# Local attention: one output projection for two units, bias products over the full height, transposes and low part moved, two mask copies on VectorE

## The chip, the core and the metric

The kernel runs on one core of a Trainium2 chip. A core has TensorE (PE, matrix products into PSUM), VectorE (DVE), ScalarE (ACT), GpSimd (POOL) and SyncE (SP, which issues DMAs). Each engine works through its own queue in order; between engines there are only semaphores. The metric is device time in microseconds, lower is better.

## The reference

Two layers, each a cross-attention and a feed-forward network, on `x` of shape (16, 64, 512). Only the first, the local attention, is touched:

```
x = x + _L0_xattn_ref(_layernorm(x, axis=-1), ctx_4096, Wq, bq, Wk, bk, Wv, bv, Wo, bo)

B, C, T = x.shape                      # 16, 64, 512
H, W = (HEADS, WINDOW)                 # 8, 16
q = _pointwise(Wq, bq, x)              # einsum('oc,bct->bot', W, t) + b
k = _pointwise(Wk, bk, cond)
v = _pointwise(Wv, bv, cond)
k = jnp.pad(k, ((0, 0), (0, 0), (pad_left, pad_right)))      # 8 and 7
v = jnp.pad(v, ((0, 0), (0, 0), (pad_left, pad_right)))
idx = jnp.arange(T)[:, None] + jnp.arange(W)[None, :]
dots = jnp.einsum('bhdt,bhdtw->bhtw', qh, k_win) * scale
attn = jax.nn.softmax(dots, axis=-1)
out = jnp.einsum('bhtw,bhdtw->bhdt', attn, v_win)
return _pointwise(Wo, bo, out)
```

Behind it come a gated feed-forward network, a cross-attention of 32 heads and a routed feed-forward network. The gated one begins with the layer norm of the rows that local attention leaves, transposed.

## The kernel before

`X` lies in SBUF as eight tiles; a tile holds two batches, 2 x 64 channels, on the 128 partitions, and 512 time steps. A tile has four units of 128 time steps, so there are 32 units, and each unit has eight blocks of 16 time steps with the 32 keys that their windows touch.

`window_attention` is a pipeline written out by hand: step n does something for several units at once, on each engine in the order in which `step` is written. With q = n mod 4 (called step 0 to step 3 of a tile here):

- TensorE: in step 0 the query projection of the next tile (L404), in step 1 its key projection (L392), both into the bank `PJ`; in step 3 four transposes of the layer-normed row of the tile t - 2 for the next stage (L233), also into `PJ`. Then in every step: value products of unit n - 3 (L444, two of 128 columns), and for the first and last unit of a tile, at the edge of the time axis, one more with `less` and `bv_row`, of one partition (L446), that takes the bias out of padded keys; the mask and score products of unit n (L451, L457), the output projection of unit n - 5 (L481, four of 128 columns), and the products of probabilities and values of unit n - 4 (L493).
- VectorE: transposition of scores to keys (L587), maximum (L590), the add into `X` with the output bias (L599); a step later sum (L566) and reciprocal (L571), another step later the transposition of probabilities (L580). Besides, per tile: layer-norm statistics of finished rows in step 1 (L198), the normed row at the start of step 2 (L222, `norm.normalise`, into `qT`), the normed `xn` for a later query projection at the start of step 3 (L528), and the low part of the transposed row at the end of step 3 (L245, `norm.low`).
- GpSimd: subtraction of the maximum (L663), product with the reciprocal (L670).
- ScalarE: exponential (L707), copies of values and of heads out of PSUM (L701, L731), biases, the high part of the transposed row (L239), and the masked copies of the query, eight per tile, one per head, from `qp` into `qx` (L722; three in step 1, three in step 2, two in step 3).

Value products and output projection share PSUM bank 6 (`VT`, `AO`), so the next value product waits for the X add (`x_added`). The query projection waits for the low part (`low_done`), since both use `PJ`. The diff touches `window_attention` alone.

Of the kernel before, what the change touches and what calls it, by code (L numbers as in the profile page):

```python
# [279 lines left out]
def window_attention(nc, sh, d, norm, ffn):  # L280
# [9 lines left out]
    STEPS = (-4, UNITS + 6, 8, UNITS_PER_TILE)  # L290
    HH = WH // 2
    FIRST = 2
    SHARERS = 3
    with ExitStack() as st:
# [17 lines left out]
        less = sb("wa_less", [1, 2, P])  # L312
        bv_row = sb("wa_bv_row", [1, P])
# [4 lines left out]
        oh = sb("wa_oh", [P, 2, HH, UNIT_T])  # L318
# [8 lines left out]
        AO = sh.PS[:, 6, 256:256 + UNIT_T]  # L327
# [3 lines left out]
        def context_due(n):  # L331
# [6 lines left out]
                 "q_mm k_mm q_biased q_ready k_ready edges bv_loaded sc_mm masks_ready keyed maxed subbed exped summed recip probs "  # L338
# [3 lines left out]
        with nc.Block() as block:  # L342
            @block.sync
            def _(sp):
                def load(dst, name, done, a, b):
                    sp.dma_start(dst[:, a:b, :], d[name][2 * a:2 * b, :, :].rearrange("(t b) s e -> (b s) t e", b=2)
                                 ).then_inc(done[a], 16)

                load(sh.X, "x", x_loaded, *LOADS[0])
                sp.dma_start(sh.const[:], d["consts"][:, :C_BASE]).then_inc(S["const_loaded"], 16)  # L350
                for i, w in enumerate(("Wq", "Wk", "Wv", "Wo")):
                    sp.dma_start(wrow[:, i, :], d["L0_" + w]).then_inc(S["loaded"], 16)
                    sp.dma_start(brow[i:i + 1, :], d["L0_b" + w[1]].rearrange("(a c) -> a c", a=1)).then_inc(S["loaded"], 16)
                load(sh.CTX, "ctx", ctx_loaded, *LOADS[0])
                for b2 in range(2):
                    sp.dma_start(bv_row[:, b2 * SEQ:(b2 + 1) * SEQ], d["L0_bv"].rearrange("(a c) -> a c", a=1)
                                 ).then_inc(S["bv_loaded"], 16)
# [12 lines left out]
            def _(pe):  # L370
# [23 lines left out]
                def step(n, u, t):  # L394
# [18 lines left out]
                    if q == 3 and live(t - 2, TT - 1):  # L413
                        if live(t + 1, TT):
                            pe.wait_ge(S["k_ready"], t + 2)
                        else:
                            pe.wait_ge(norm.low_done, t - 1)
                        norm.transpose(pe, t - 2, u // 4, PJ)

                    if live(n, UNITS):  # L420
                        pe.wait_ge(S["q_ready"], t + SHARERS)
                        pe.wait_ge(S["k_ready"], t + 1)
                        if not isinstance(n, int) or n >= 1:
                            pe.wait_ge(S["keyed"], n)
                        else:
                            pe.wait_ge(S["masks_ready"], 2)

                    m, w = n - 3, (u - 3) % 8
                    if live(m, UNITS):
# [7 lines left out]
                        if not isinstance(n, int) or m >= 3:  # L437
                            pe.wait_ge(S["x_added"], m - 2)
# [25 lines left out]

                    m = n - 4
# [6 lines left out]
                    m = n - 5  # L472
                    if live(m, UNITS):
                        pe.wait_ge(S["oh_copied"], m + 1)
                        pe.wait_ge(S["vt_copied"], m + 3 if live(m + 2, UNITS) else UNITS)
                        if not isinstance(n, int) or m >= 1:
                            pe.wait_ge(S["x_added"], m)
# [32 lines left out]
            def _(vec):  # L510
# [43 lines left out]
                def step(n, u, t):  # L554
# [6 lines left out]
                    if q == 1 and live(t - 2, TT - 1):  # L561
                        vec.wait_ge(S["x_added"], 4 * t - 4)
# [31 lines left out]
                    m, w = n - 5, (u - 5) % 4  # L594
                    if live(m, UNITS):
                        vec.wait_ge(S["ao_mm"], m + 1)
                        x = sh.X[:, bass.ds(t - 1 if q >= 1 else t - 2, 1),
                                 w * UNIT_T:(w + 1) * UNIT_T]
                        nc.vector.scalar_tensor_tensor(x, AO.rearrange("p (a e) -> p a e", a=1), bias[:, 3:4], x,  # L599
                                                       ALU.add, ALU.add).then_inc(S["x_added"], 1)  # L600

# [16 lines left out]
            def _(gp):  # L618
# [6 lines left out]
                nc.gpsimd.memset(wT[:], 0.0).then_inc(S["zeroed"], 1)  # L625
                nc.gpsimd.memset(blank[:], 0.0).then_inc(S["zeroed"], 1)
# [6 lines left out]
                nc.gpsimd.memset(less[:, 0, 0:PAD], -1.0).then_inc(S["padded"], 1)  # L633
                nc.gpsimd.memset(less[:, 1, P - PAD:], -1.0).then_inc(S["padded"], 1)
# [47 lines left out]
            def _(act):  # L682
# [8 lines left out]
                def step(n, u, t):  # L691
# [17 lines left out]
                    if live(t + 1, TT):  # L709
                        if q == 0:  # L710
                            if isinstance(t, int) and t == 0:
                                act.wait_ge(S["q_ready"], SHARERS)
                            add_bias(t + 1, 0, "q_mm", qp[:], "q_biased")
# [13 lines left out]
                    if live(m, UNITS):  # L727
                        act.wait_ge(S["oh_mm"], m + 1)
                        if not isinstance(n, int) or m >= 2:
                            act.wait_ge(S["ao_mm"], m - 1)  # L730
                        nc.scalar.activation(oh[:, u % 2, :, :].rearrange("p h (i x) -> p i h x", i=4),  # L731
# [1325 lines left out]
```

## Time and profile before

| | us |
|---|---|
| median of 3 runs | 1130.06 (1130.03 to 1131.46) |
| the profiled execution | 1132.62 |
| its span in the profile | 1130.8 |
| TensorE busy | 1045.0 (92%) |
| VectorE busy | 661.4 (58%) |
| GpSimd busy | 514.7 (46%) |
| ScalarE busy | 352.3 (31%) |

Local attention ends at 173.3 us, and the rest of the span belongs to the three later stages. In the rows further down, a timeline row gives the start and the length in us, the engine, the source line, the operation, what it writes and reads, and in brackets how long its engine stood idle before it and what ended that. PEld is the load of stationary operands. An f32 product appears in two records for each instruction. The start of an instruction can lie a little before the end of the one before it on the same engine, so distances between starts say what an instruction costs its engine.

### The profile page before, as it was taken

What the parts mean: (1) busy time and instruction counts of PE and PEld (TensorE: products, weight loads), DVE (VectorE), ACT (ScalarE), POOL (GpSimd) and SP (SyncE); (2) the same over time, 40 slices, a digit from 0 to 9 for tenths busy, and PEclk for the clock granted to TensorE, in tenths of its full rate; (3) what the DMA queues carried; (4) which work ended last, traced back from release to release, by engine and by line L of the source; (5) the groups of instructions that cost most, each with busy time, mean ns of one, the idle gap of its engine ahead of it and who ended that gap; (6) DMA issues with size and microseconds to landing.
All of it is one profiled execution on the core that took longest, in us unless ns stands there. A gap on an engine that the chain in (4) does not pass through costs nothing. (4 is left out here: it accounts for less than half of the span.)

```text
span 1130.8 us, 24015 instructions
## 1 busy us (share of the span) xinstructions
PE 1045.0 (92%) x9170; PEld 869.1 (77%) x9170; DVE 661.4 (58%) x1357; ACT 352.3 (31%) x826; POOL 514.7 (46%) x594
## 2 busy tenths in 40 slices
PE   6899988999999889999999999999999999745993
PEld 3677777888887678888888888888888888534783
DVE  4799873544544675656555565656555666741324
ACT  3677743222222323222222222222222222211331
POOL 3555531422123365445454454444544442337755
PEclk9899998999999889999999999999999999976997
DMA  7100006656450021111011110011010000036768
GB/s 237 23 3 4 4 4 177 209 192 212 151 205 30 29 72 33 47 29 48 29 33 51 31 46 30 29 48 29 28 57 29 29 10 1 1 129 213 242 215 270
DMA packets 51806, 92.07 MB, mean 81 GB/s; under 512 B 10748, under 2 KB 24316, under 8 KB 51260
## 3 DMA queue, kind: packets, MB, share of 16 engines
q1 hardware_dynamic: 42108, 69.13, 19.4%
q10 hardware_dynamic: 6624, 12.06, 3.1%
q0 software_dynamic: 2976, 9.44, 2.5%
q8 instruction: 76, 1.25, 0.5%
q14 instruction: 22, 0.18, 0.0%
HBM read 77.25 MB, written 36.18 MB: 100 GB/s over the span
## 5 line engine op out<-in xcount | busy, mean ns | idle before, releaser
L121 PE MATMUL PS<-NTh,W 128*128 128x256 f32 (+2 forms) x688 | 217.1, 315 | 0.0
L122 PE MATMUL PS<-NTl,W 128*128 128x256 f32 (+2 forms) x688 | 214.2, 311 | 0.0
L123 PE MATMUL PS<-NTh,W 128*128 128x256 f32 (+2 forms) x688 | 214.2, 311 | 0.0
L122 PEld LDWEIGHTS PS<-NTl,W 128*128 128x128 f32 (+1 forms) x688 | 131.3, 191 | 7.0
L123 PEld LDWEIGHTS PS<-NTh,W 128*128 128x128 f32 (+1 forms) x688 | 129.4, 188 | 8.6
L121 PEld LDWEIGHTS PS<-NTh,W 128*128 128x128 f32 (+1 forms) x688 | 129.6, 188 | 7.2
L1507 POOL TENSOR_TENSOR W<-ca_raw,W 128x512 fp32r<-128x512 f32 x64 | 82.6, 1292 | 109.7 <-ACT W L1354 109.7
L1445 DVE TENSOR_REDUCE ca_su<-room 128x4 f32<-128x256 f32 x64 | 26.8, 419 | 154.0 <-ACT room L1379 154.0
L1474 DVE TENSOR_TENSOR room<-PS,ca_sinT 64x512 f32<-64x512 f32 (+1 forms) x192 | 115.0, 599 | 2.6
L121 PE MATMUL PS<-W,ca_aTh 128*128 128x512 f32 x256 | 106.9, 417 | 3.1 <-DVE X L1462 3.1
L122 PE MATMUL PS<-W,ca_aTh 128*128 128x512 f32 x256 | 101.3, 396 | 0.0
L123 PE MATMUL PS<-W,ca_aTl 128*128 128x512 f32 x256 | 100.9, 394 | 0.0
L1379 ACT ACTIVATE room<-room 128x256 f32<-128x256 f32 x64 | 26.8, 419 | 227.1 <-POOL room L1557 227.1
L1547 POOL TENSOR_TENSOR qT<-room 128x512 f32<-128x512 f32 x64 | 81.7, 1277 | 29.1 <-DVE room L1474 27.7
L1474 DVE TENSOR_TENSOR room<-PS,ca_cosT 128x512 f32<-128x512 f32 (+1 forms) x96 | 57.8, 602 | 56.8 <-PE PS L1293 56.4
L1044 POOL TENSOR_TENSOR ff_hl<-ff_hf,W 128x512 fp32r<-128x512 f32 (+1 forms) x22 | 28.6, 1302 | 132.9 <-ACT W L939 132.9
L1000 DVE TENSOR_TENSOR X<-X,PS 128x512 f32<-128x512 f32 x88 | 60.3, 686 | 48.8 <-PE PS L123 48.3
L1403 ACT ACTIVATE room<-PS 128x256 f32<-128x256 f32 x64 | 24.6, 385 | 186.1 <-PE PS L1319 186.1
L121 PE MATMUL PS<-ca_wkvh,CTh 128*128 128x256 f32 x256 | 79.3, 310 | 2.2 <-issue 2.2
L1534 POOL TENSOR_TENSOR room<-room,ca_rc 128x256 f32<-128x256 f32 x64 | 39.3, 613 | 76.7 <-DVE ca_rc L1447 76.7
L123 PE MATMUL PS<-ca_wkvh,CTl 128*128 128x256 f32 x256 | 72.4, 283 | 0.0
L122 PE MATMUL PS<-ca_wkvl,CTh 128*128 128x256 f32 x256 | 72.1, 282 | 0.0
(253 smaller groups left out, 2354.4 us busy)
## 6 DMA issues: line engine op xcount, KB each, us to landing
ca_raw<-in_L_Wq SPq DMA_DIRECT2D x32, 256.0 KB, 2.8
ca_raw<-in_L_Wo SPq DMA_DIRECT2D x32, 256.0 KB, 2.6
rf_raw<-in_experts SPq DMA_DIRECT2D x28, 256.0 KB, 4.3
room<-slots ACTq DMA_DIRECT2D x23, 256.0 KB, 3.4
outs<-room ACTq DMA_DIRECT2D x23, 256.0 KB, 3.3
outs<-blank SPq DMA_DIRECT2D x11, 512.0 KB, 8.8
room<-in_L_Wg SPq DMA_DIRECT2D x10, 256.0 KB, 2.9
room<-in_L_Wu SPq DMA_DIRECT2D x10, 256.0 KB, 3.1
```

What stands on the lines that cost most here:

```text
L121: nc.tensor.matmul(out, l_hi, r_hi, start=first, stop=False)
L122: nc.tensor.matmul(out, l_hi, r_lo, start=False, stop=False)
L123: return nc.tensor.matmul(out, l_lo, r_hi, start=False, stop=last)
L1000: nc.vector.tensor_tensor(sh.X[:, t, :], sh.X[:, t, :], D[:, t % 4, :], ALU.add).then_inc(S["added"], 1)
L1044: nc.gpsimd.tensor_tensor(hl[:w, slot, tok], hf[:w, half, :], hh[:w, slot, tok].bitcast(F32), ALU.subtract).then_inc(S["h_split"], 1)
L1379: nc.scalar.activation(s, s, ACT.Exp).then_inc(S["exped"], 1)
L1403: nc.scalar.activation(pT, PP, ACT.Copy).then_inc(S["pp_copied"], 1)
L1445: nc.vector.reduce_sum(su[:, w, :], sm[:, w, :, :], AX_X).then_inc(S["summed"], 1)
L1474: return nc.vector.tensor_tensor(out[out_rows, some].rearrange("p (m k) -> p m k", m=count), x[rows, :].rearrange("p (m k) -> p m k", m=co ...
L1507: return nc.gpsimd.tensor_tensor(dst[1], src, dst[0].bitcast(F32), ALU.subtract)
L1534: nc.gpsimd.tensor_tensor(s, s, rc[:, w, :].unsqueeze(2).broadcast_to([P, 4, SEQ]), ALU.mult).then_inc(S["probs"], 1)
L1547: last = nc.gpsimd.tensor_tensor(qT[:, slot, j, :, :].rearrange("p b (m q) -> p m b q", m=2), *parts, ALU.add)
```

## The change

- Output projection and X add are done for two units at once, in steps 0 and 2 of a tile (`pair_due(n)`: the pair p = (n - 6) / 2 at even n). `oh` holds two units side by side, `AO` is 256 columns wide. The value products wait for `x_added` only in odd steps.
- `less` and `bv_row` have 128 partitions, all zero but the first; GpSimd sets `bv_row` to zero, and SyncE waits for that (`bv_zeroed`) before the two loads of the bias.
- The four transposes of the normed row are issued in step 2, between the scores and the output projection, and no longer at the start of step 3.
- The low part stands ahead of the keys' transposition in step 3, and no longer behind the maximum.
- Two of the eight masked query copies are made by VectorE at the end of step 2 (semaphore `q_others`); ScalarE makes two in each of the steps 1 to 3.

```diff
+    PAIR_T = 2 * UNIT_T
+    def pair_due(n):
+        return (n - 6) // 2 if n % 2 == 0 and 0 <= n - 6 < UNITS else None
...
-        less = sb("wa_less", [1, 2, P])
-        bv_row = sb("wa_bv_row", [1, P])
+        less = sb("wa_less", [P, 2, P])
+        bv_row = sb("wa_bv_row", [P, P])
...
-        oh = sb("wa_oh", [P, 2, HH, UNIT_T])
+        oh = sb("wa_oh", [P, 2, HH, PAIR_T])
...
-        AO = sh.PS[:, 6, 256:256 + UNIT_T]
+        AO = sh.PS[:, 6, 256:256 + PAIR_T]
...
+                sp.wait_ge(S["bv_zeroed"], 1)
...
-                    if q == 3 and live(t - 2, TT - 1):
-                        if live(t + 1, TT):
-                            pe.wait_ge(S["k_ready"], t + 2)
-                        else:
-                            pe.wait_ge(norm.low_done, t - 1)
-                        norm.transpose(pe, t - 2, u // 4, PJ)
...
-                        if not isinstance(n, int) or m >= 3:
-                            pe.wait_ge(S["x_added"], m - 2)
+                        if pair_due(n - 1) is not None:
+                            pe.wait_ge(S["x_added"], pair_due(n - 1) + 1)
...
+                    if q == 2 and live(t - 2, TT - 1):
+                        if live(t + 1, TT):
+                            pe.wait_ge(S["k_ready"], t + 2)
+                        else:
+                            pe.wait_ge(norm.low_done, t - 1)
+                        norm.transpose(pe, t - 2, u // 4, PJ)
...
-                            last = nc.tensor.matmul(AO, wo[:, h, :], oh[:, (u - 5) % 2, h, :], start=h == 0, stop=h == HH - 1)
+                            last = nc.tensor.matmul(AO, wo[:, h, :], oh[:, p % 2, h, :], start=h == 0, stop=h == HH - 1)
...
+                    if q == 3 and live(t - 2, TT - 1):
+                        norm.low(vec, t - 2, PJ)
+
...
-                    if q == 3 and live(t - 2, TT - 1):
-                        norm.low(vec, t - 2, PJ)
...
+                    p = pair_due(n)
+                    if p is not None:
+                        vec.wait_ge(S["ao_mm"], p + 1)
+                        x = sh.X[:, p // 2, p % 2 * PAIR_T:(p % 2 + 1) * PAIR_T]
+                        nc.vector.scalar_tensor_tensor(x, AO, bias[:, 3:4], x, ALU.add, ALU.add).then_inc(S["x_added"], 1)
+
+                    if q == 2 and live(t + 1, TT) and t >= 0:
+                        vec.wait_ge(S["q_biased"], t + 2)
+                        if t >= 1:
+                            vec.wait_ge(S["sc_mm"], 4 * t)
+                        for h in range(WH - 2, WH):
+                            last = nc.vector.tensor_scalar(qx[:, 1 - slot, :, h, :], qp[:].rearrange("p (k t) -> p k t", t=BLK), hm[:, h:h + 1],
+                                                           None, ALU.mult)
+                        last.then_inc(S["q_others"], 1)
...
-                        for h in range(3 * q - 3, min(3 * q, WH)):
+                        for h in range(2 * q - 2, 2 * q) if t >= 0 else range(3):
```

The line numbers shift by the added lines: L587 becomes L599, L590 L602, L599 L607, L566 L575, L571 L580, L580 L589, L528 L537, L404 L411, L392 L399, L444 and L446 become L446 and L448, L457 L459, L481 L490, L493 L502; the mask copies on VectorE are L614, and the helpers L198, L222, L233 and L245 keep theirs. The mask and score products L451 and L457 become L453 and L459.

VectorE in a steady tile, from the keys of step 1 to the sum of step 2, before:

```order
L587 STREAM_TRANSPOSE wa_sm<-PS 128x512
L590 TENSOR_REDUCE wa_mx<-wa_sm 128x16
L599 SCALAR_TENSOR_TENSOR X<-PS,wa_bias,X 128x128
L222 TENSOR_SCALAR qT<-X,norm_mv,norm_rstd 128x512
L566 TENSOR_REDUCE wa_su<-wa_sm 128x16
```

The same place of the changed kernel:

```order
L599 STREAM_TRANSPOSE wa_sm<-PS 128x512
L602 TENSOR_REDUCE wa_mx<-wa_sm 128x16
L222 TENSOR_SCALAR qT<-X,norm_mv,norm_rstd 128x512
L575 TENSOR_REDUCE wa_su<-wa_sm 128x16
L580 RECIPROCAL wa_rc<-wa_su 128x16
```

The add is gone from step 1, and the normed row follows the maximum directly.

VectorE in the same tile, from the keys of step 2 to the sum of the next step 0, before:

```order
L587 STREAM_TRANSPOSE wa_sm<-PS 128x512
L590 TENSOR_REDUCE wa_mx<-wa_sm 128x16
L599 SCALAR_TENSOR_TENSOR X<-PS,wa_bias,X 128x128
L528 TENSOR_SCALAR wa_xn<-X,wa_mv,wa_rstd 128x512
L566 TENSOR_REDUCE wa_su<-wa_sm 128x16
L571 RECIPROCAL wa_rc<-wa_su 128x16
L580 STREAM_TRANSPOSE wa_pt<-wa_sm 128x512
L587 STREAM_TRANSPOSE wa_sm<-PS 128x512
L590 TENSOR_REDUCE wa_mx<-wa_sm 128x16
L245 TENSOR_TENSOR NTl<-PS,NTh 128x4x128
L599 SCALAR_TENSOR_TENSOR X<-PS,wa_bias,X 128x128
L566 TENSOR_REDUCE wa_su<-wa_sm 128x16
```

The same place of the changed kernel:

```order
L599 STREAM_TRANSPOSE wa_sm<-PS 128x512
L602 TENSOR_REDUCE wa_mx<-wa_sm 128x16
L607 SCALAR_TENSOR_TENSOR X<-PS,wa_bias,X 128x256
L614 TENSOR_SCALAR wa_qx<-wa_qp,const 128x32x16 x2
L537 TENSOR_SCALAR wa_xn<-X,wa_mv,wa_rstd 128x512
L575 TENSOR_REDUCE wa_su<-wa_sm 128x16
L580 RECIPROCAL wa_rc<-wa_su 128x16
L589 STREAM_TRANSPOSE wa_pt<-wa_sm 128x512
L245 TENSOR_TENSOR NTl<-PS,NTh 128x4x128
L599 STREAM_TRANSPOSE wa_sm<-PS 128x512
L602 TENSOR_REDUCE wa_mx<-wa_sm 128x16
L575 TENSOR_REDUCE wa_su<-wa_sm 128x16
```

The two copies have come in behind a wider add, the low part has moved from behind the maximum to ahead of the keys, and the add of step 3 is gone.

TensorE in steps 2 and 3 of a steady tile, before (`PS` is PSUM; the first row is the value product of step 2):

```order
L444 MATMUL PS<-wa_wT,CTX 128x128
L444 MATMUL PS<-wa_wT,wa_edge 128x128
L446 MATMUL PS<-wa_bv_row,wa_less 128x128
L451 MATMUL PS<-wa_exact_band,wa_exact_id 128x256 x2
L457 MATMUL PS<-wa_qx,wa_kp 32x128 x16
L481 MATMUL PS<-wa_oh,wa_wo 128x128 x4
L493 MATMUL PS<-wa_pt,wa_vt 32x4x16 x32
L233 MATMUL PS<-const,qT 128x128 x4
L444 MATMUL PS<-wa_wT,wa_edge 128x128
L446 MATMUL PS<-wa_bv_row,wa_less 128x128
L444 MATMUL PS<-wa_wT,CTX 128x128
```

The same place of the changed kernel:

```order
L446 MATMUL PS<-wa_wT,CTX 128x128
L446 MATMUL PS<-wa_wT,wa_edge 128x128
L448 MATMUL PS<-wa_bv_row,wa_less 128x128
L453 MATMUL PS<-wa_exact_band,wa_exact_id 128x256 x2
L459 MATMUL PS<-wa_qx,wa_kp 32x128 x16
L233 MATMUL PS<-const,qT 128x128 x4
L490 MATMUL PS<-wa_oh,wa_wo 128x256 x4
L502 MATMUL PS<-wa_pt,wa_vt 32x4x16 x32
L446 MATMUL PS<-wa_wT,wa_edge 128x128
L448 MATMUL PS<-wa_bv_row,wa_less 128x128
L446 MATMUL PS<-wa_wT,CTX 128x128
```

The transposes have moved ahead of a projection of 256 columns.

## Rows read from the trace of the kernel before

**Rows 1.** Busy us of each engine by stretch, granted clock (PEclk), DMA.
```profile
core 0: us, PE busy (x) PEld busy (x) DVE busy (x) ACT busy (x) POOL busy (x), PEclk, DMA share, GB/s
21.00:39.00 18.00, 10.88 (x206) 6.69 (x185) 14.17 (x31) 9.11 (x16) 9.19 (x10) 0.73 0.57 148
39.00:54.50 15.50, 15.35 (x441) 11.65 (x413) 12.97 (x25) 11.71 (x22) 8.80 (x10) 0.99 0.02 4
54.50:140.00 85.50, 82.96 (x2258) 64.17 (x2257) 78.91 (x149) 63.66 (x115) 46.26 (x55) 1.00 0.01 4
```

**Rows 2.** Timeline of TensorE at the end of the first tile.
```profile
34.41 2.05 PE L404 MATMUL PS<-wa_xn,wa_wT 128*128 128x512 f32 x2 [3.30 <-DVE wa_xn L528]
```

**Rows 3.** Timeline of TensorE in one steady tile: start, length, line.
```profile
103.82 1.10 PE L404 MATMUL PS<-wa_xn,wa_wT 128*128 128x512 f32 x2 [0.37 <-issue]
...
106.12 1.16 PE L481 MATMUL PS<-wa_oh,wa_wo 128*128 128x128 f32 x8
107.21 0.85 PE L493 MATMUL PS<-wa_pt,wa_vt 32*32 32x64 f32 x64
108.00 1.12 PE L392 MATMUL PS<-CTX,wa_wT 128*128 128x512 f32 x2
108.96 0.61 PE L444 MATMUL PS<-wa_wT,CTX 128*128 128x128 f32 x4
109.32 0.48 PE L451 MATMUL PS<-wa_exact_band,wa_exact_id 128*128 128x256 f32 x2
109.73 0.67 PE L457 MATMUL PS<-wa_qx,wa_kp 64*32 64x128 f32 x32
...
112.35 0.46 PE L444 MATMUL PS<-wa_wT,CTX 128*128 128x128 f32 x2
113.38 0.50 PE L451 MATMUL PS<-wa_exact_band,wa_exact_id 128*128 128x256 f32 x2
...
121.07 1.10 PE L404 MATMUL PS<-wa_xn,wa_wT 128*128 128x512 f32 x2 [0.37 <-issue]
```

**Rows 4.** Timeline of VectorE in the same tile.
```profile
110.51 0.72 DVE L587 STREAM_TRANSPOSE wa_sm<-PS 128x512 f32<-128x512 f32 x1
111.26 0.69 DVE L590 TENSOR_REDUCE wa_mx<-wa_sm 128x16 f32<-128x512 f32 x1
111.86 0.34 DVE L599 SCALAR_TENSOR_TENSOR X<-PS,wa_bias,X 128x128 f32<-128x128 f32 x1
112.12 1.23 DVE L222 TENSOR_SCALAR qT<-X,norm_mv,norm_rstd 128x512 f32<-128x512 f32 x1
113.28 0.67 DVE L566 TENSOR_REDUCE wa_su<-wa_sm 128x16 f32<-128x512 f32 x1
...
115.43 0.69 DVE L590 TENSOR_REDUCE wa_mx<-wa_sm 128x16 f32<-128x512 f32 x1
...
117.45 0.67 DVE L566 TENSOR_REDUCE wa_su<-wa_sm 128x16 f32<-128x512 f32 x1
...
118.93 0.72 DVE L587 STREAM_TRANSPOSE wa_sm<-PS 128x512 f32<-128x512 f32 x1
...
120.28 0.68 DVE L245 TENSOR_TENSOR NTl<-PS,NTh 128x512 fp32r<-128x512 f32 x1
```

**Rows 5.** VectorE's copies beside GpSimd's work: timeline, and ns min/median/max of one line.
```profile
112.03 1.05 POOL L663 TENSOR_TENSOR wa_sm<-wa_sm,wa_mx 128x512 f32<-128x512 f32 x1 [0.79 <-DVE wa_mx L590]
...
16.39 0.49 DVE L535 TENSOR_SCALAR wa_qx<-wa_qp,const 128x512 f32<-128x512 f32 x1 [2.90 <-ACT wa_qp L685]
16.79 1.31 DVE L535 TENSOR_SCALAR wa_qx<-wa_qp,const 128x512 f32<-128x512 f32 x2
16.45 2.10 POOL L645 TENSOR_SCALAR wa_qx<-wa_qp,const 128x512 f32<-128x512 f32 x1 [8.57 <-ACT wa_qp L685]
...
L222 DVE TENSOR_SCALAR qT<-X,norm_mv,norm_rstd x20: 536/548/1236, 60.3 to 995.6; 128x512 f32<-128x512 f32 x20
L645 POOL TENSOR_SCALAR wa_qx<-wa_qp,const x2: 1572/1838/2103, 16.5 to 18.6; 128x512 f32<-128x512 f32 x2
```

More of the change, by code:

```diff
@@ L337, in window_attention @@
         names = ("const_loaded loaded zeroed padded ct_tr ct_hi ct_lo w_tr w_ready wo_ready stats aggr veps power_set rstd normed "
-                 "q_mm k_mm q_biased q_ready k_ready edges bv_loaded sc_mm masks_ready keyed maxed subbed exped summed recip probs "
+                 "q_mm k_mm q_biased q_ready q_others k_ready edges bv_zeroed bv_loaded sc_mm masks_ready keyed maxed subbed exped summed recip probs "
                  "rowed vt_mm vt_copied oh_mm oh_copied ao_mm x_added").split()
@@ L354, in _ @@
                 load(sh.CTX, "ctx", ctx_loaded, *LOADS[0])
+                sp.wait_ge(S["bv_zeroed"], 1)
                 for b2 in range(2):
-                    sp.dma_start(bv_row[:, b2 * SEQ:(b2 + 1) * SEQ], d["L0_bv"].rearrange("(a c) -> a c", a=1)
+                    sp.dma_start(bv_row[0:1, b2 * SEQ:(b2 + 1) * SEQ], d["L0_bv"].rearrange("(a c) -> a c", a=1)
                                  ).then_inc(S["bv_loaded"], 16)
@@ L412, in step @@
                                 stay_busy(nc, sh.PS[:, 0, :], ident, sh.X[:, 0, :], 1)
[L413 to L418 removed]
                     if live(n, UNITS):
                         pe.wait_ge(S["q_ready"], t + SHARERS)
+                        if t >= 1:
+                            pe.wait_ge(S["q_others"], t)
                         pe.wait_ge(S["k_ready"], t + 1)
@@ L470, in step @@
                             pe.wait_ge(S["oh_copied"], m)
[L472 to L477, printed above, removed]
+                    p = pair_due(n)
+                    if p is not None:
+                        pe.wait_ge(S["oh_copied"], 2 * p + 2)
+                        pe.wait_ge(S["vt_copied"], min(n - 2, UNITS))
+                        if p >= 1:
+                            pe.wait_ge(S["x_added"], p)
                         else:
@@ L561, in step @@
                     if q == 1 and live(t - 2, TT - 1):
-                        vec.wait_ge(S["x_added"], 4 * t - 4)
+                        vec.wait_ge(S["x_added"], 2 * t - 2)
                     m, w = n - 2, (u - 2) % 4
@@ L590, in step @@
                         nc.vector.reduce_max(mx[:, u % 4, :], sm[:, u % 4, :, :], AX_X).then_inc(S["maxed"], 1)
-                    if q == 3 and live(t - 2, TT - 1):
-                        norm.low(vec, t - 2, PJ)
[L594 to L600, printed above, removed]
+                    p = pair_due(n)
+                    if p is not None:
+                        vec.wait_ge(S["ao_mm"], p + 1)
[3 more added lines that the diff above has]
+                        vec.wait_ge(S["q_biased"], t + 2)
+                        if t >= 1:
+                            vec.wait_ge(S["sc_mm"], 4 * t)
[3 more added lines that the diff above has]
+                        last.then_inc(S["q_others"], 1)
                     if n in range(3):
@@ L625, in _ @@
                 nc.gpsimd.memset(wT[:], 0.0).then_inc(S["zeroed"], 1)
+                nc.gpsimd.memset(bv_row[:], 0.0).then_inc(S["bv_zeroed"], 1)
                 nc.gpsimd.memset(blank[:], 0.0).then_inc(S["zeroed"], 1)
@@ L632, in _ @@
                 gp.wait_ge(S["padded"], 4)
-                nc.gpsimd.memset(less[:, 0, 0:PAD], -1.0).then_inc(S["padded"], 1)
-                nc.gpsimd.memset(less[:, 1, P - PAD:], -1.0).then_inc(S["padded"], 1)
+                nc.gpsimd.memset(less[0:1, 0, 0:PAD], -1.0).then_inc(S["padded"], 1)
+                nc.gpsimd.memset(less[0:1, 1, P - PAD:], -1.0).then_inc(S["padded"], 1)
                 gp.wait_ge(S["padded"], 6)
@@ L712, in step @@
                                 act.wait_ge(S["q_ready"], SHARERS)
+                            if isinstance(t, int) and t >= 1:
+                                act.wait_ge(S["q_others"], t)
                             add_bias(t + 1, 0, "q_mm", qp[:], "q_biased")
@@ L728, in step @@
                         act.wait_ge(S["oh_mm"], m + 1)
-                        if not isinstance(n, int) or m >= 2:
-                            act.wait_ge(S["ao_mm"], m - 1)
-                        nc.scalar.activation(oh[:, u % 2, :, :].rearrange("p h (i x) -> p i h x", i=4),
+                        if m >= 4:
+                            act.wait_ge(S["ao_mm"], (m - 4) // 2 + 1)
+                        nc.scalar.activation(oh[:, m // 2 % 2, :, m % 2 * UNIT_T:(m % 2 + 1) * UNIT_T].rearrange("p h (i x) -> p i h x", i=4),
                                              OH.rearrange("p i (h x) -> p i h x", h=HH), ACT.Identity,
```

## The prediction

> **What bounds the kernel now.** I read the table of busy time by stretch first. Local attention is the first 173 of 1130.8 us, and it splits into a first tile (21 to 39 us), a second, a steady part (54.5 to 140) and a drain. In the steady part TensorE is busy 82.96 and VectorE 78.91 of 85.50 us, at the full clock [rows 1]. Two engines that full, one waiting for the other in turn, mean a loop through both. So next I laid out one steady tile from the timeline: TensorE's query projection (L404) starts at 103.82 and again at 121.07, a period of 17.25 us [rows 3]. Following who starts right behind whom gives the loop:
>
> - TensorE, 103.82 to 109.73: query projection, value product, scores, output projection (L481, 1.09 to the next product), probability product (L493), key projection, value product, start of step 1's scores: 5.91 [rows 3].
> - The scores release VectorE's transposition L587 at 110.51, 0.78 later. From there VectorE never waits: L590 (0.75 on), L599 (0.60), L222 (0.26), L566 (1.16), and so on through steps 2 and 3 to L245 at 120.28 [rows 4].
> - L245 takes 0.68; 0.79 after its start the next L404 starts (they share a PSUM bank): 5.91 + 0.78 + 9.77 + 0.79 = 17.25. The reader should see that the period is this sum, and that each edit is worth what it does to the loop, not to a busy share.
>
> **The change on the loop of a steady tile.**
>
> (a) *Paired projection, step 0.* L481 at 128 columns becomes half as many groups of 256. A group now takes 1.09 [rows 3]. Low end: still 1.09, if the stationary loads set it. High end: twice, 2.18. The nearest row is the key projection L392: the same f32 product over 512 columns, two passes in 0.96 [rows 3], or 0.48 a pass; a 256-column pass is half, 0.24, and four products have eight: 1.92. That 0.48 holds half of a changeover from the small score tiles which a group pays once, so I take 1.80. Over a tile TensorE saves 4 x 1.09 - 2 x 1.80 = 0.76, but the loop passes one group, in step 0, now the longer one: **+0.71**.
>
> (b) *No add in step 1.* The X add runs only in steps 0 and 2, so L599 (0.26 to the next start) leaves the loop in front of L222. More hangs on it. L222 has 1.24 us where its shortest is 0.54 [rows 5]: GpSimd's subtraction L663 starts at 112.03, L222 at 112.12, and L222's successor only at 113.28, 0.20 behind the end of the subtraction (113.08) [rows 4, 5]. So L222 is held until GpSimd is done. The subtraction starts 0.77 behind the start of L590 (111.26), the add 0.60 behind it. With the add gone L222 stands in the add's place, 0.17 before the subtraction. Which of the two then waits is shown at one place: mask copy L535 starts at 16.39, GpSimd's L645 at 16.45, and the copy takes its 0.49 undisturbed while L645 takes 2.10 against 1.57 for the shortest [rows 5]. First come, first served. L222 then costs the distance of two such copies that start at 16.39 and 16.79, 0.40, less the small difference of contiguous output, say 0.37, for 1.16: 0.26 + 0.79 = **-1.05**. The subtraction is put back by about 0.35; its exponential is wanted only by the sum a step later, some 4 us on.
>
> The Trainium skill has this as a rule (SBUF — State Buffer, "Who interferes with whom"): a VectorE instruction in a two-port mode and a GpSimd instruction share a port pair under an exclusive lock, and the one that issues first blocks the other. By that rule L222, 0.17 ahead, is free and (b) is -1.05; by L222's own rows of the steady part, 1.24 each time, it would stay held and (b) would be -0.26. By the same rule the mask copies of (c) are held, which is against this change.
>
> (c) *Two mask copies on VectorE, step 2.* They stand behind the add and ahead of the layer-norm row of L528. GpSimd's subtraction runs by then, so the first is held as L528 was: before, from L590 (115.43) through L599 and the held L528 to L566 (117.45) are 2.02 [rows 4]; now these 2.02 hold the add and the first copy, and the second (0.40) and L528 (0.37) follow free. **+0.77**. The wider add has 0.13 more (128 columns more at about 1 ns, from L599's 0.34 and the 0.68 of 512-column rows such as L245) and its wait for the later projection some tenths; both end inside the hold. Bounds of the second copy: 0.40, and 0.81, the distance between the copies at 16.79 and the next one, when GpSimd was at work [rows 5]: 16.79 and 1.31 for the two, less the last one's 0.49. GpSimd has no work queued there, so 0.40. ScalarE loses two of eight copies and was waiting anyway: nothing.
>
> (d) *Low part ahead of the keys, transposes in step 2.* The loop leaves VectorE at the end of L245. Before, L587 and L590 stood in front of it: 118.93 to 120.28 [rows 4]. **-1.35**. Next late is VectorE's own way on: L245, keys, maximum, sum, reciprocal, transposition, keys takes 0.68 + 0.75 + 0.60 + 0.74 + 0.17 + 0.58 = 3.5, against 0.75 + 2.5 through the query projection, then some 4.1 to step 1's keys, 7.6, where the loop takes 0.75 + 5.91 + 0.71 + 0.78 = 8.2. So the loop still leads, by 0.6, and the full 1.35 is to be had. On TensorE the four transposes (0.49) move from before step 3's value product to between step 2's scores and its projection. That delays the pair's projection, for which the add is queued, and behind the add both copies and L528; the add becomes ready about 0.9 behind the start of the maximum, before the hold of (c) ends at 1.82. Nothing. ScalarE's high part stands where it stood, ready some 1.5 us before L245.
>
> (e) *Full-height bias products.* An interior step spends 108.96 to 109.32, 0.36, on two value products; an edge step with the one-row bias product 112.35 to 113.38, 1.03 [rows 3]. Three alike would be 0.54; I take 0.60 (low end 0.54, high end 1.03). Two per tile, in steps 2 and 3, where TensorE is ahead of VectorE: nothing on the steady loop, 0.4 each in the drain.
>
> Steady tile: 17.25 + 0.71 - 1.05 + 0.77 - 1.35 = 16.33; laid out step by step with the waits it comes to 16.4. The new waits in front of step 0's add (some 0.3, for the longer projection) lie in the 0.6 of VectorE's slack.
>
> **Sum over the stage.** First tile: L404 for the second tile is held 3.30 us by L528 [rows 2], behind the statistics that follow step 2 on VectorE; the two copies go ahead of them, +0.80. Second tile (no layer-norm row yet): bound by TensorE, three single projections against one pair, 3 x 1.09 - 1.80: -1.5. Third to sixth: 4 x -0.9. Seventh: it had no L528 and so paid no hold in step 2 before, and (c) costs 0.4 more: -0.5. Last tile and drain: nine single groups against five pairs, 9.8 - 9.0 = -0.8; three edges, -1.2; the last add, wider and behind a longer pair, +0.2. In all 0.8 - 1.5 - 3.6 - 0.5 - 1.8 = **-6.6**. The start is untouched: the added memset of `bv_row` is one of 0.5 us at most on GpSimd by 2 us, and SyncE reaches the wait at 6.3. The later stages start when local attention ends, and keep their length. Span 1130.8 - 6.6 = 1124.2. The profiled execution took 1132.62, so 2.56 above the median of 1130.06; the gain is set against the median: **1123.4**.
>
> **Rivals.**
>
> *L222 stays held* (if VectorE asks for the port only once the maximum before it has drained, 0.69 behind its start, a lead of 0.17 is nearly gone). The add's 0.26 and the hold come back, 1.05 in tiles 2 to 7: 6 x 1.05 = 6.3, so 1129.7. For it: no row of this trace has a row-norm starting first. Against: 16.39. This is no change.
>
> *Slower: the port everywhere.* Decides if GpSimd's work wins whenever it starts near a VectorE copy. L222 held (+6.3), and each second mask copy at 0.81 instead of 0.40, both copies so in the first two tiles: 5 x 0.41 + 2 x 0.82 = 3.7. 1123.4 + 6.3 + 3.7 = 1133.4. It turns from gain to loss once holds eat more than 6.6 us.
>
> *The pair costs two singles* (2.18): 0.38 a group on the loop in six tiles and five groups at 0.38 in the drain, 4.2: 1127.6. *The clock*: 21 to 39 us has a mean of 0.73, the steady part 1.00 [rows 1]; the first stretch at 1.2 GHz followed TensorE's long waits. TensorE will be idle some 1.2 us a tile instead of 0.5, always in short pieces. A stretch of the lower level in the steady part would cost about what the first tile has over its parts, 2 us: 1125.4, and it can move the other way. *The change does not do what it says* (a pair undone, a copy elsewhere) is ruled out by the order of instructions.
>
> **Chances and range.** Forecast 0.62 (own range 1121.0 to 1126.0, from a pair at 1.70 to 1.92 and the edges at 1.03); L222 held 0.18; slower by the port 0.10, by another cause 0.02; dear pair 0.05; a clock stretch 0.03. The range must reach the L222 case and its small additions: 1121.0 to 1131.0, leaving out the slower cases and a tail below. A measurement here tells 0.2%, 2.3 us, from no change: faster is below 1127.8 and holds the forecast, dear pair and clock cases, 0.70; same is the L222 case, 0.18; slower 0.12.
>
> **What would show it.** The row-norm's duration in the steady part: 0.55 right, 1.24 the rival, with GpSimd's subtraction starting behind it and longer. The first mask copy about 1 us, the second 0.5. The pair's eight passes to the next group: 1.7 to 1.9. Edge steps 0.6 against 1.03. The low part directly before the keys, and the query projection right behind it. Period 16.3 to 16.5, and the first tile longer. I am wrong if the period stays above 17, or if it falls but a later stage gives it back.

## The result, and the profile after

The changed kernel takes 1129.14 us (median of 20 runs, 1125.32 to 1132.8) beside 1132.06 for the kernel before on the same chips. The ratio is 0.9976, 95% interval 0.9965 to 0.9987: 2.7 us less, between 1.5 and 4.0. The forecast was 6.6 us less. The sign held and the time lies in the stated range; the size did not hold.

Two profiled executions are compared by stage, not by span: behind local attention the span has 957.5 us before and 959.9 after, though nothing there was touched, and in another profile of the changed kernel 957.0. So "stage" is taken from VectorE's first transposition of scores to the end of the last X add, and the "period" of a tile from the keys of its step 0 to those of the next:

| us | before | after | forecast of the difference | measured |
|---|---|---|---|---|
| first tile | 17.50 | 18.29 | +0.8 | +0.79 |
| second | 15.60 | 14.00 | -1.5 | -1.60 |
| third to sixth | 17.25 to 17.29 | 16.58 to 16.60 | 4 x -0.9 | -2.70 |
| seventh | 16.71 | 16.14 | -0.5 | -0.57 |
| last tile and drain | 33.06 | 33.05 | -1.8 | -0.01 |
| stage | 151.93 | 147.84 | -6.6 | -4.09 |

Everything up to the seventh tile came within 0.9 us of the forecast. The drain gave nothing. Busy time by stretch, of after (the counterpart of [rows 1]):

```profile
core 0: us, PE busy (x) PEld busy (x) DVE busy (x) ACT busy (x) POOL busy (x), PEclk, DMA share, GB/s
21.00:39.00 18.00, 8.61 (x148) 4.90 (x148) 15.28 (x34) 8.20 (x14) 10.33 (x13) 0.78 0.54 147
39.00:54.50 15.50, 14.89 (x431) 11.20 (x429) 11.76 (x22) 10.95 (x20) 7.22 (x10) 0.92 0.02 5
54.50:140.00 85.50, 80.43 (x2254) 60.20 (x2253) 77.83 (x155) 58.34 (x107) 50.00 (x58) 1.00 0.02 4
```

TensorE is now busy 94% of the steady part instead of 97%. One steady tile of after, VectorE from the keys of step 1 to the keys of step 3 (the counterpart of [rows 4]):

```profile
93.70 0.72 DVE L599 STREAM_TRANSPOSE wa_sm<-PS 128x512 f32<-128x512 f32 x1 [0.23 <-PE PS L459]
94.45 0.69 DVE L602 TENSOR_REDUCE wa_mx<-wa_sm 128x16 f32<-128x512 f32 x1
95.06 0.54 DVE L222 TENSOR_SCALAR qT<-X,norm_mv,norm_rstd 128x512 f32<-128x512 f32 x1
95.51 0.68 DVE L575 TENSOR_REDUCE wa_su<-wa_sm 128x16 f32<-128x512 f32 x1
...
97.67 0.69 DVE L602 TENSOR_REDUCE wa_mx<-wa_sm 128x16 f32<-128x512 f32 x1
98.88 0.48 DVE L607 SCALAR_TENSOR_TENSOR X<-PS,wa_bias,X 128x256 f32<-128x256 f32 x1 [0.52 <-PE PS L490]
99.28 0.89 DVE L614 TENSOR_SCALAR wa_qx<-wa_qp,const 128x512 f32<-128x512 f32 x2
100.08 0.54 DVE L537 TENSOR_SCALAR wa_xn<-X,wa_mv,wa_rstd 128x512 f32<-128x512 f32 x1
100.54 0.67 DVE L575 TENSOR_REDUCE wa_su<-wa_sm 128x16 f32<-128x512 f32 x1
...
102.00 0.65 DVE L245 TENSOR_TENSOR NTl<-PS,NTh 128x512 fp32r<-128x512 f32 x1
102.57 0.69 DVE L599 STREAM_TRANSPOSE wa_sm<-PS 128x512 f32<-128x512 f32 x1
```

TensorE and GpSimd in the same tile (of [rows 3] and [rows 5]):

```profile
86.15 1.10 PE L411 MATMUL PS<-wa_xn,wa_wT 128*128 128x512 f32 x2 [0.26 <-issue]
...
88.48 1.99 PE L490 MATMUL PS<-wa_oh,wa_wo 128*128 128x256 f32 x8
90.40 0.85 PE L502 MATMUL PS<-wa_pt,wa_vt 32*32 32x64 f32 x64
...
92.93 0.67 PE L459 MATMUL PS<-wa_qx,wa_kp 64*32 64x128 f32 x32
...
94.78 0.46 PE L446 MATMUL PS<-wa_wT,CTX 128*128 128x128 f32 x2 [0.40 <-DVE wa_sm L599]
...
95.44 0.48 PE L453 MATMUL PS<-wa_exact_band,wa_exact_id 128*128 128x256 f32 x2
...
102.75 1.10 PE L411 MATMUL PS<-wa_xn,wa_wT 128*128 128x512 f32 x2 [0.58 <-issue]
```
```profile
95.22 1.28 POOL L679 TENSOR_TENSOR wa_sm<-wa_sm,wa_mx 128x512 f32<-128x512 f32 x1 [0.98 <-DVE wa_mx L602]
```

The same loop as before closes with the new numbers: TensorE from the query projection to step 1's scores 6.78 (86.15 to 92.93; it was 5.91), 0.77 to the keys, VectorE from there to L245 8.30 (93.70 to 102.00; it was 9.77), 0.75 to the next query projection. The sum is 16.60, the period.

### The profile page after: what moved, and what is told of

Read it like the earlier page. It is cut to its first block and busy times, and to the rows that moved or that the text cites. A ratio compares the mean times of both kernels' runs of the same rounds, so it can differ in the third digit from the quotient of the medians.

```text
span 1131.0 us, 23724 instructions
## 1 busy us (share of the span) xinstructions
PE 1037.8 (92%) x9042; PEld 860.1 (76%) x9042; DVE 658.2 (58%) x1355; ACT 343.7 (30%) x812; POOL 516.2 (46%) x595
## 3 DMA queue, kind: packets, MB, share of 16 engines
q8 instruction: 75, 1.23, 0.5%
```

## The experiments

Each is the changed kernel with one edit, or the kernel before with one part of the change. Ratios are against the kernel before on the same chip.

**The drain.** This is where the forecast and the profile part. TensorE of after at the end of the stage:

```profile
159.38 0.39 PE L448 MATMUL PS<-wa_bv_row,wa_less 128*128 128x128 f32 x2
162.48 0.63 PE L233 MATMUL PS<-const,qT 128*128 128x128 f32 x4 [2.72 <-DVE qT L222]
162.95 1.89 PE L490 MATMUL PS<-wa_oh,wa_wo 128*128 128x256 f32 x8
```

The transposes of the last row, moved a step sooner, make TensorE wait 2.72 us for the normed row, and the paired projection is queued behind them. In the first experiment only this row's transposes go back to their old step:

```diff
+                    if q == 3 and t == TT:
+                        pe.wait_ge(norm.low_done, t - 1)
+                        norm.transpose(pe, t - 2, u // 4, PJ)
...
-                    if q == 2 and live(t - 2, TT - 1):
+                    if q == 2 and t < TT and live(t - 2, TT - 1):
```

> The changed kernel, but the last row's four transposes (of the seventh tile, in the drain behind the last unit) stand where they stood before, at the start of the next step; nothing else differs. Theory (the drain's gain was lost because these transposes, one step sooner, make TensorE wait 2.72 us for a row that VectorE norms only behind its context work): TensorE's idle time before that L233 goes to below 0.3, drain from the last tile's first keys to the last add 31.0 instead of 33.05, period unchanged at 16.59, time 2.0 us below the changed kernel's. Rival (another wait, say for the probabilities, takes its place): drain 32.8 to 33.1, time the same.

Measured: 1125.5 us, ratio 0.9936 (0.9917 to 0.9955); drain 30.99. It was repeated on another chip, unaltered, beside the changed kernel, also unaltered:

> The changed kernel once more, beside the next run on one chip. Its profile gave an attention stage shorter by 4.1 us than the kernel before, its times a gain of 2.7 us. If the profile's value holds, the ratio is 0.996 (1128.0 beside 1132.5); if the times' value holds, 0.9976 again (1129.8). The stage in the profile should come out at 147.8 us again, with a drain of 33.05, whatever the start does; the first keys stand at 21.0 to 21.7 or at 23.2 to 23.3, and the theory that this start goes with the stretches of lower clock and not with the edit expects either.

> The last row's transposes at their old step, as in e1_drain_late, beside the changed kernel on the same chip. The theory (the moved transposes of the last row hold TensorE ahead of the paired projection) expects 2.06 us less in the drain, so about 0.998 of the changed kernel's time, and a drain of 31.0 us. The rival (e1's gain was the lower-clock stretch that was missing behind its stage, and not the drain) expects a drain of 31.0 too, but a time that differs from the changed kernel's by more or less than 2.1 us according to where the stretches fall.

The changed kernel took 1129.16 us (ratio 0.997, 0.9955 to 0.9985), its profile has a stage of 147.47 and a drain of 32.77; its first keys stand at 21.14, where they were at 23.29 in the first profile, so the late start was not the edit. The late transposes gave 1123.7 us (0.9918, 0.9898 to 0.9939), drain 30.61. TensorE there waits 1.00 us instead of 2.72, and for the probabilities that the projection's group needs anyway:

```profile
156.52 0.39 PE L452 MATMUL PS<-wa_bv_row,wa_less 128*128 128x128 f32 x2
157.91 1.99 PE L494 MATMUL PS<-wa_oh,wa_wo 128*128 128x256 f32 x8 [1.00 <-DVE wa_pt L593]
...
161.55 0.60 PE L233 MATMUL PS<-const,qT 128*128 128x128 f32 x4
```

So the moved transposes cost 2.06 and 2.16 us of drain in the two pairs of profiles. About 0.2 of that comes back in the seventh tile, which is 16.32 and 16.33 long with the late transposes and 16.14 and 16.13 without; over the stage the first pair differs by 1.83, the second by 2.09 (0.15 of it in the first tile). The times differ by more, 1129.16 to 1123.7 on one chip: my 0.998 of the changed kernel's time was missed, it was 0.995. One difference beyond the drain is the clock just behind the stage. The 20 us after the last add, in the second profile of the changed kernel and in that of the late transposes:

```profile
168.60:188.60 20.00, 16.99 (x79) 13.90 (x80) 6.88 (x13) 7.59 (x12) 3.75 (x8) 0.91 0.77 218
```
```profile
166.20:186.20 20.00, 16.80 (x85) 13.60 (x86) 7.58 (x14) 7.79 (x12) 4.84 (x9) 1.00 0.80 224
```

A granted clock of 0.91 is the lower level, 1.2 GHz, for part of the stretch; I estimate that 0.09 of 20 us, 1.8 us of work, is lost by it. Both profiles with the late transposes have 1.00 there, both of the changed kernel 0.91. 2.2 and 1.8 would make 4.0 of 5.5, and the intervals of the two ratios leave about 3 us of room. But the whole of what follows the stage is equal in this pair (957.0 and 956.9 us), so the profiles do not show that these 1.8 us reach the end. What the times gain beyond the drain stays open.

**The port.** A VectorE instruction of 0.28 us is put ahead of L222, so that GpSimd's subtraction starts first again:

```diff
+                    if q == 1 and live(t - 2, TT - 1) and live(n, UNITS):
+                        nc.vector.reduce_max(scratch[:], ident.rearrange("p (a k) -> p a k", a=4), AX_X)
                     p = pair_due(n)
```

> The changed kernel with one more small instruction on VectorE (a maximum over 128 columns of a constant into a scratch tile, about 0.3 us) between the maximum of step 1 and the normed row L222, in the place of the add that the change took out there. Theory (port, first come first served: with it GpSimd's subtraction starts first again): L222 back at 1.24 us, subtraction back at 1.05, period 16.59 + 0.26 + 0.79 = 17.6, time 6 to 7 us above the changed kernel's. Rival (L222 was freed by something else, such as an emptier queue): L222 stays at 0.54, period 16.9, time 1.6 us above.

```profile
95.94 0.28 DVE L605 TENSOR_REDUCE wa_scratch<-const 128x4 f32<-128x128 f32 x1
96.14 1.30 DVE L222 TENSOR_SCALAR qT<-X,norm_mv,norm_rstd 128x512 f32<-128x512 f32 x1
97.36 0.67 DVE L576 TENSOR_REDUCE wa_su<-wa_sm 128x16 f32<-128x512 f32 x1
...
99.52 0.69 DVE L603 TENSOR_REDUCE wa_mx<-wa_sm 128x16 f32<-128x512 f32 x1
100.12 0.47 DVE L610 SCALAR_TENSOR_TENSOR X<-PS,wa_bias,X 128x256 f32<-128x256 f32 x1
100.52 1.50 DVE L617 TENSOR_SCALAR wa_qx<-wa_qp,const 128x512 f32<-128x512 f32 x2
101.94 0.53 DVE L538 TENSOR_SCALAR wa_xn<-X,wa_mv,wa_rstd 128x512 f32<-128x512 f32 x1
102.39 0.67 DVE L576 TENSOR_REDUCE wa_su<-wa_sm 128x16 f32<-128x512 f32 x1
```
```profile
96.11 1.05 POOL L682 TENSOR_TENSOR wa_sm<-wa_sm,wa_mx 128x512 f32<-128x512 f32 x1 [0.98 <-DVE wa_mx L603]
```

L222 starts 0.03 behind the subtraction and is held to 1.30; in after it starts 0.16 ahead, takes 0.54, and the subtraction 1.28 instead of 1.05. The steady period is 17.55, 0.96 longer, and the time 1135.66 us, ratio 1.0018 (1.0003 to 1.0033). This is the rival "L222 stays held" made to happen, with 0.28 us of another instruction in the place of the add. It was priced at 6.3 us. In the profile the stage is 6.8 us longer than in after (154.66), of which the four steady tiles have 3.8 and the seventh tile and the drain the rest; by the two ratios the time is about 4.8 us longer, less than the forecast 6 to 7. The rows also show step 2: here the add waits for nothing and the copies are held, 1.42 from the start of the first to L538; in after the add waits 0.52 and the copies take 0.80. From the maximum to the sum both take 2.87 us. So the wait for the projection takes the place of the hold and costs nothing beyond it, as forecast, but with nothing to spare.

**The low part.** Back behind the maximum, all else as changed:

```diff
-                    if q == 3 and live(t - 2, TT - 1):
-                        norm.low(vec, t - 2, PJ)
...
                         nc.vector.reduce_max(mx[:, u % 4, :], sm[:, u % 4, :, :], AX_X).then_inc(S["maxed"], 1)
+                    if q == 3 and live(t - 2, TT - 1):
+                        norm.low(vec, t - 2, PJ)
```

> The changed kernel with the low part (L245) behind the maximum of step 3 again, ahead of nothing. Theory ((d) is worth 1.35 a tile on the loop): period 17.9, stage 5.3 us longer than the changed kernel's, so the whole gain and more is this edit's, time 2 us above the kernel before. Rival (the other edits would carry the gain alone, TensorE being ahead): period 16.6 to 16.9.

Measured: 1138.65 us, ratio 1.0052 (1.0035 to 1.0069), stage 157.77. By stretch from one query projection to the next:

```profile
68.89:88.34 19.45, 17.30 (x437) 12.91 (x437) 15.27 (x31) 11.45 (x21) 9.59 (x12) 0.91 0.01 3
88.34:106.26 17.92, 15.57 (x437) 11.75 (x437) 15.28 (x31) 11.34 (x21) 9.58 (x12) 1.00 0.02 4
106.26:125.71 19.45, 17.30 (x436) 12.85 (x437) 15.27 (x31) 11.45 (x21) 9.58 (x12) 0.91 0.01 3
```

At the full clock the tile costs 17.92, 1.33 more than in after: (d)'s 1.35. The expected 5.3 us for the stage are these 1.33 four times; it came out 9.9 longer, and the time 5.9 us above the kernel before by the ratio, not 2. The rest is clock. Two tiles have a stretch at 1.2 GHz and cost 1.53 on top each. They are the ones that begin behind TensorE's longer waits for the query projection (1.91 and 1.92 us, against 1.16 and 1.14 for the others). In the drain, behind a wait of 2.72, the pair's eight passes take 3.30 instead of 1.82, another 1.5. The forecast had such a stretch at 0.03 chance and as one event.

Alone on the kernel before, the same move is worth much less:

```diff
+                    if q == 3 and live(t - 2, TT - 1):
+                        norm.low(vec, t - 2, PJ)
+
                     if live(n, UNITS):
...
-                    if q == 3 and live(t - 2, TT - 1):
-                        norm.low(vec, t - 2, PJ)
```

> The kernel before, with one edit: the low part (L245) ahead of the keys' transposition in step 3; all the rest as before. Theory: on the loop of the kernel before it takes the keys and the maximum (1.35) from the way to the query projection, but VectorE's own order is now next (its work in a tile, 16.4 of 17.25, has hardly any idle left), so only 0.4 to 0.5 a tile: period 16.8, time 2 to 3 us below before. Rival (the ledger's full 1.35): period 15.9, 7 us below.

Measured: ratio 0.9966 (0.9954 to 0.9979), a period of 16.84, so 0.42 less. Its steady part, and the end of the low part beside the next query projection:

```profile
54.50:140.00 85.50, 84.97 (x2333) 66.01 (x2332) 80.51 (x154) 64.11 (x116) 47.70 (x56) 1.00 0.02 4
```
```profile
100.39 0.65 DVE L245 TENSOR_TENSOR NTl<-PS,NTh 128x512 fp32r<-128x512 f32 x1
```
```profile
101.32 0.85 PE L493 MATMUL PS<-wa_pt,wa_vt 32*32 32x64 f32 x64
102.11 1.13 PE L404 MATMUL PS<-wa_xn,wa_wT 128*128 128x512 f32 x2
```

L404 starts 1.72 behind L245 instead of 0.79, right behind L493: TensorE, busy 84.97 of 85.50 us, is the bound by itself. The expectation had the size right and the reason wrong: it named VectorE's own order. Note also that this one move, with a stage of 149.03, is as good as the whole change by the times (0.9966 and 0.9976, with intervals that overlap) and only 1.2 us behind it by the stage.

**The pair alone**, on the kernel before: paired projection and add, without (c), (d) and (e).

```diff
-                    if live(m, UNITS):
+                    p = pair_due(n)
+                    if p is not None:
...
-                            last = nc.tensor.matmul(AO, wo[:, h, :], oh[:, (u - 5) % 2, h, :], start=h == 0, stop=h == HH - 1)
+                            last = nc.tensor.matmul(AO, wo[:, h, :], oh[:, p % 2, h, :], start=h == 0, stop=h == HH - 1)
```

> The kernel before with the paired projection and add alone (transposes in step 3, low part behind the maximum, eight copies on ScalarE, bias products of one partition). Theory: the loop passes the long group (1.92 for 1.09) while TensorE is still late, and both groups of a tile are on it, with the low part still late: period 18.0 to 18.5, time 1 to 6 us above before although TensorE does less work. Rival (the ledger's terms add: +0.83 for (a), -1.05 for (b)): period 17.0, time 2 us below.

Measured: slower, ratio 1.0032 (1.0021 to 1.0044), period 18.51, though L222 takes 0.54.

```profile
99.50 0.54 DVE L222 TENSOR_SCALAR qT<-X,norm_mv,norm_rstd 128x512 f32<-128x512 f32 x1
...
102.11 0.69 DVE L597 TENSOR_REDUCE wa_mx<-wa_sm 128x16 f32<-128x512 f32 x1
103.65 0.48 DVE L605 SCALAR_TENSOR_TENSOR X<-PS,wa_bias,X 128x256 f32<-128x256 f32 x1 [0.85 <-PE PS L488]
...
106.98 0.72 DVE L594 STREAM_TRANSPOSE wa_sm<-PS 128x512 f32<-128x512 f32 x1 [0.94 <-PE PS L464]
```

The add waits 0.85 for the projection, and step 3's keys 0.94 for scores that stand on TensorE behind the projection, the transposes and a one-row edge. By (a) and (b) alone the tile would have been 0.34 shorter; it is 1.26 longer. The terms that make it up are 0.87 for the longer group in step 0, 0.96 less for L222, 0.38 more from step 2's maximum to its sum (2.40 instead of 2.02) and the 0.94: 1.23. The edits are not additive.

**The edge.** `less` and `bv_row` with one partition again, all else as changed:

```diff
-        less = sb("wa_less", [P, 2, P])
-        bv_row = sb("wa_bv_row", [P, P])
+        less = sb("wa_less", [1, 2, P])
+        bv_row = sb("wa_bv_row", [1, P])
```

> The changed kernel with less and bv_row of one partition again. Theory: an edge step's value products take 1.03 instead of 0.66; on the steady loop 0 to 0.2 a tile, in the drain 0.7, time 0.7 to 2 us above the changed kernel. Rival (the narrow product never was the price): 0.66 stays, no difference.

```profile
98.97 0.69 DVE L602 TENSOR_REDUCE wa_mx<-wa_sm 128x16 f32<-128x512 f32 x1
100.47 0.48 DVE L607 SCALAR_TENSOR_TENSOR X<-PS,wa_bias,X 128x256 f32<-128x256 f32 x1 [0.81 <-PE PS L490]
```

Ratio 0.9995 (0.998 to 1.001), period 16.95 to 17.08. The add stands 1.50 behind the maximum instead of 1.21, and each steady tile is 0.36 to 0.5 longer, more than the expected 0 to 0.2; the drain is 0.27 longer, less than the expected 0.7. The stage is 150.60, 2.76 longer than in after. So the full height is worth two thirds of the stage's gain of 4.1. By the two ratios it is 2.2 of the 2.7 us, but their intervals overlap, so the times alone don't show it.

**The mask copies**, all on ScalarE again (the block on VectorE and the waits on `q_others` removed):

```diff
-                        for h in range(2 * q - 2, 2 * q) if t >= 0 else range(3):
+                        for h in range(3 * q - 3, min(3 * q, WH)):
```

> The changed kernel with all eight masked query copies of a tile on ScalarE again (three, three, two). Ledger of the prediction, (c) is +0.77 of the loop: period 15.8, first tile 0.8 shorter. Theory now (part of the 0.77 lies in a wait of the add for the longer paired projection, and the norm of the next xn is then held by GpSimd itself, as before the change): period 16.2 to 16.3, first tile 17.5 instead of 18.3, in all 1 to 2.5 us below the changed kernel. Rival (ScalarE's third copy delays values and heads): period 16.6 or more, no gain.

Ratio 0.9967 (0.9948 to 0.9985), not to be told from 0.9976. The profile points the other way than the expectation: the stage is 150.42, 2.6 us longer than in after. The first tile is 17.49, 0.80 shorter as forecast, but the second 15.37, 1.37 longer. There the pair starts 6.75 behind the tile's first keys instead of 6.13, since it waits for ScalarE's copy of the values, which is the rival's reason, and TensorE then stands still for 0.69 in the middle of a group, waiting for nothing that the profile shows:

```profile
47.47 1.97 PE L488 MATMUL PS<-wa_oh,wa_wo 128*128 128x256 f32 x8 [0.84 <-ACT wa_vt L707]
...
53.28 0.36 PE L500 MATMUL PS<-wa_pt,wa_vt 32*32 32x64 f32 x20 [0.69 <-issue]
```

The steady tiles alternate between 16.3, as expected and 0.29 shorter than in after, and 17.08. In the drain the last row's transposes wait 3.08 us, and behind them the pair's eight passes take 3.30 us at the lower clock, 1.5 us of the loss. In the longer tiles TensorE stands still again:

```profile
85.45 0.72 PE L500 MATMUL PS<-wa_pt,wa_vt 32*32 32x64 f32 x48
86.69 0.34 PE L500 MATMUL PS<-wa_pt,wa_vt 32*32 32x64 f32 x16 [0.51 <-issue]
```

Last, the late transposes together with mask copies on VectorE only from the second tile on:

```diff
-                    if q == 2 and live(t + 1, TT) and t >= 0:
+                    if q == 2 and live(t + 1, TT) and t >= 1:
```

> The changed kernel with the last row's transposes late, as in the run before, and with the eight copies of the first tile's step 0 to 3 all on ScalarE (VectorE makes its two only from the second tile on). Theory ((c) is dear in the first tile, where the copies stand ahead of the statistics on which all waits): first tile 17.5 instead of 18.3, everything else as with the transposes late, time 0.8 us below that kernel's, 7.5 us below before. Rival (ScalarE's third copy holds the first tile as much): first tile 18.3.

Ratio 0.9931 (0.9919 to 0.9944), stage 146.01, the same as without the edit: first tile 0.80 shorter, second 0.81 longer. 0.54 of that is again a standstill:

```profile
51.15 0.36 PE L506 MATMUL PS<-wa_pt,wa_vt 32*32 32x64 f32 x20 [0.54 <-issue]
```

## Why the prediction was right in sign and wrong in size

**The step that failed** is in (d): "On TensorE the four transposes (0.49) move ... Nothing." That was worked out for the steady tile and holds there. The sum over the stage then used the drain's terms (-0.8, -1.2, +0.2) without asking again where the moved transposes stand in the drain, where the normed row of the seventh tile comes late and the paired projection is queued behind them. With the transposes late the drain is 2.07 and 2.45 us shorter than before, so the sum of those terms (-1.8) came out; the move cost 2.1 and took all of it. It is the only term by which the forecast misses more than a microsecond. The terms singly are not borne out: the kernel with the pair alone, one-row edges and all, already has a drain of 30.92, 2.14 shorter, where -0.8 and +0.2 were forecast for the pair, and one-row edges in the changed kernel lengthen its drain by 0.27, where the three edges were put at 1.2. That the sum fits is in part luck.

"Holds there" is as much as the port experiment shows: from step 2's maximum to its sum are 2.87 whether the add waits for the projection or not. No run puts the transposes of the steady tiles back by themselves.

**The range.** That 1129.14 lies in it is luck too. The upper end was set to take in the case of a held L222 (1129.7), and the time came out there, above the 1127.8 below which the forecast had its 0.70, although L222 ran free at 0.54.

**(a)** The pair was taken at 1.80 and takes 1.92 (88.48 to 90.40), the value that the key projection's row gave. The deduction for a changeover was wrong. On the loop TensorE's part grew by 0.87, not 0.71.

**(b)** right in mechanism, 0.96 for 1.05. L222 to its successor is 0.45 (95.06 to 95.51), not 0.37. The two mask copies 0.40 apart were the right row, but an instruction with a normed row's operands takes 0.05 more, not less. The Trainium skill's rule (SBUF — State Buffer, "Who interferes with whom"), that whoever issues first gets the port pair for the whole instruction, is borne out by the 0.54 with a lead of 0.16 and the 1.30 with a lag of 0.03.

**(c)** 2.87 from the maximum to the sum, where 2.79 was forecast. The two copies end when they were said to, and L537 takes 0.46 in place of 0.37, the same slip as in (b). But the first copy is not held, as its sign (about 1 us) asked: the two take 0.80 together, and the add in front of them waits 0.52 for the projection. The add was to be ready 0.9 behind the maximum and starts 1.21 behind it, which used up the slack of the hold; the hold itself shows in the port experiment, 1.42. As the worth of (c), 0.77 is too much: with all copies on ScalarE a tile without a standstill is 0.29 shorter, 16.30, of which TensorE is busy 15.76.

**(d)** From step 2's sum to L245 are 1.46 (100.54 to 102.00) instead of 2.83: 1.37 for the 1.35 forecast, and 1.33 a tile when undone. But the check on what is late next looked only at VectorE's own way. The kernel alone with this edit shows the true next bound, TensorE's own work, 16.74 us a tile by [rows 1] (82.96 x 17.25 / 85.50). In the changed kernel TensorE's work is 15.6 us a tile (80.43 x 16.60 / 85.50), since the pair and the edges shorten it too, and that leaves room for the full gain.

**(e)** An edge takes 0.66 where the prediction took 0.60. "Nothing on the steady loop" was wrong: once the add waits for the pair, TensorE's work ahead of the pair in step 2 has no slack left, and what is added to it is on the loop, 0.36 or more a tile. It is no miss in the sum, since the forecast's step times assumed the short edge, but as the worth of the edit it is.

**The steady tile** by its terms: +0.87 - 0.96 + 0.85 - 1.37 - 0.04 = -0.65, against -0.9: four tiles make 0.9 us of miss. With 1.8 in the drain that makes 2.7, and the other tiles give back 0.2: the difference between -6.6 and -4.1 in the profile. The rest, from -4.1 (-4.5 in the second profile) to the -2.7 of the times, belongs to no step of the prediction, and no run shows its cause: the second set of times gave -3.4 (-5.1 to -1.7), and what follows the stage differs by up to 6.4 us from one profile to another.

## What to carry to other kernels

An instruction moved in a pipeline has one price per part of the pipeline: work out the steady tile, and then the first and the last again, for every instruction in the queue behind the moved one. Before a gain on a loop through two engines is booked, compare it with the busy time of each of them per tile. That bound is not in the loop's own sum: here it cut 1.35 to 0.42. Judge parts of a change together: the pair alone lost 0.3%, the low part alone won 0.3%, and all of it with the last row's transposes left where they were won 0.6 and 0.8%, more than the changed kernel's 0.2 and 0.3%.

## What the hardware showed that was not expected

- A product with one partition between full-height ones costs more than one with 128. The edge step of three products, from its first to the next mask product, takes 0.66 at full height (94.78 to 95.44) and 1.03 with the one-row product [rows 3]; in the edge experiment, which changes nothing else, it is 1.02 (95.99 to 97.01).
- TensorE stands still for 0.16 to 0.69 us in the middle of a group of small products, with no semaphore to wait for. The place goes with the program and not with the time: 17 instructions before the end of the same group at 118.92 us in one profile of the changed kernel and at 116.69 in the other. In the mask experiment it recurs every 33.4 us, two tiles. None was seen in the local attention of the kernel before, nor in that of the changed kernel with one-row edges. Its cause is not shown; it takes back gains of half a microsecond.

```profile
118.92 0.35 PE L502 MATMUL PS<-wa_pt,wa_vt 32*32 32x64 f32 x17 [0.26 <-issue]
```
```profile
116.69 0.35 PE L502 MATMUL PS<-wa_pt,wa_vt 32*32 32x64 f32 x17 [0.24 <-issue]
```

- The part of the span behind the stage, the same code in every kernel, took between 953.5 and 959.9 us from one profile to the next. The granted clock of a few stretches differs between them; how much of the spread that makes is not shown. The spread, 6.4 us, is larger than the gain.
